# A two-layer graph network kernel on one core: every engine's order of steps and the order of the shared PSUM banks chosen anew

## The reference, cut to what matters

```
# layer 0: attention masked by adj
v, q, k = relu(x Wv + bv), relu(x Wq + bq), relu(x Wk + bk)
att = softmax((q k^T) * adj - 9e15 * (1 - adj))
x   = layernorm(x + relu((att v) Wo + bo))
# layer 1: a rank-one attention weighted by adj
h   = x W^T + b ;  e, f = h a1, h a2
u   = adj * exp(e_i + f_j + a_b)
x   = layernorm(x + (u / sum(u)) h)
```

## Time and profile before

| what | value |
|---|---|
| median of three runs | 395.15 us (395.12 to 395.23) |
| the profiled execution | 395.13 us, span 393.4 us |
| mean granted TensorE clock | 0.991 of full speed |
| busy: PE, ACT, DVE, POOL | 380.5 (97%), 329.9 (84%), 292.8 (74%), 279.9 (71%) us |
| HBM traffic | 204 GB/s over the span |

### The profile page before, as it was taken

The page is one execution under the profiler, slowest core; times in us unless marked ns, Lnnn a source line. Parts: engine busy times, 40 slices in busy tenths (PEclk is TensorE's granted clock), DMA queues, the critical chain, the costliest instruction groups (busy, mean ns, idle before and its releaser), DMA issues.

```text
span 393.4 us, 8653 instructions
## 1 busy us (share of the span) xinstructions
PE 380.5 (97%) x2757; PEld 355.2 (90%) x2757; DVE 292.8 (74%) x883; ACT 329.9 (84%) x661; POOL 279.9 (71%) x258
## 2 busy tenths in 40 slices
PE   8999999999999999999999999999999999999990
PEld 7798989989999999999999999999999999999990
DVE  3786796678668886777957887688867779697976
ACT  5877679987889887997879878898888969999962
POOL 1454951696458994789937998389956899576673
PEclk9999999999999999999999999999999999999996
DMA  8945533807657168754597266780676647978011
GB/s 259 376 166 166 164 129 137 328 38 268 200 185 314 61 235 260 262 203 171 175 292 298 84 240 215 243 322 13 253 214 233 252 162 285 386 224 282 4 55 53
DMA packets 38156, 80.71 MB, mean 205 GB/s; under 512 B 2785, under 2 KB 19681, under 8 KB 38113
## 3 DMA queue, kind: packets, MB, share of 16 engines
q1 hardware_dynamic: 37824, 80.03, 58.3%
q10 hardware_dynamic: 288, 0.14, 0.1%
HBM read 75.96 MB, written 4.19 MB: 204 GB/s over the span
## 4 chain that ended last, share of the span: by engine, by line
PE 91%; DVE 5%; issue 2%; POOL 0%; ACT 0%; POOLq 0%; DVEq 0%; ACTq 0%
PE pt_ps L1612 14%; PE m_ps L1660 13%; PE s_ps L1541 8%; PE av_ps L1625 8%; PE av_ps L1626 8%; PE av_ps L1624 8%; PE s_ps L1543 7%; PE s_ps L1542 7%; PE m_ps L1583 4%; PE m_ps L1649 3%; PE m_ps L1633 3%; PE m_ps L1541 2%; PE m_ps L1542 2%; PE m_ps L1543 2%; PE m_ps L1640 2%
## 5 line engine op out<-in xcount | busy, mean ns | idle before, releaser
L1033 DVE TENSOR_TENSOR prob_tl<-pt_ps,prob_th 128x512 fp32r<-128x512 f32 x128 | 85.5, 684 | 29.8 <-ACT prob_th L670 29.6
L1025 DVE CUSTOM_DVE_ANT_0 prob<-s_ps,penalty 128x1024 f32<-128x1024 f32 x64 | 78.0, 1218 | 30.8 <-PE s_ps L1543 26.2
L670 ACT ACTIVATE prob_th<-pt_ps 128x512 fp32r<-128x512 f32 x128 | 74.7, 596 | 21.0 <-PE pt_ps L1612 20.8
L405 POOL TENSOR_SCALAR penalty<-raw 128x1024 bf16<-128x1024 f32 x64 | 66.4, 1047 | 28.3 <-DMA raw<-in_adj_dram 13.2
L662 ACT ACTIVATE prob<-prob,neg_max 128x1024 f32<-128x1024 f32 x64 | 73.8, 1153 | 1.4 <-DVE neg_max L1025 1.3
L1624 PE MATMUL av_ps<-prob_th,vh 128*128 128x256 f32 x256 | 74.1, 290 | 0.0
L1612 PE MATMUL pt_ps<-rhs,prob 128*128 128x128 f32 x512 | 73.2, 273 | 0.0
L1626 PE MATMUL av_ps<-prob_th,vl 128*128 128x256 f32 x256 | 72.4, 283 | 0.0
L1625 PE MATMUL av_ps<-prob_tl,vh 128*128 128x256 f32 x256 | 72.4, 283 | 0.0
L607 ACT ACTIVATE adj_t<-adjt_in 128x1024 fp32r<-128x1024 f32 x56 | 59.3, 1061 | 11.2 <-PE m_ps L1660 11.1
L1612 PEld LDWEIGHTS pt_ps<-rhs,prob 128*128 128x128 f32 x512 | 60.1, 141 | 4.1
(11 more groups left out here) (139 smaller groups left out, 785.2 us busy)
## 6 DMA issues: line engine op xcount, KB each, us to landing
raw<-in_adj_dram SPq DMA_DIRECT2D x64, 512.0 KB, 5.6
adjt_in<-in_adj_t_dram SPq DMA_DIRECT2D x56, 512.0 KB, 3.9
x_in<-in_x_dram SPq DMA_DIRECT2D x8, 512.0 KB, 6.2
raw<-in_adj_t_dram SPq DMA_DIRECT2D x8, 512.0 KB, 5.7
out_dram<-out_sb SPq DMA_DIRECT2D x14, 256.0 KB, 4.5
xt_odd<-in_x_t_dram SPq DMA_DIRECT2D x8, 256.0 KB, 5.2
raw<-in_x_t_dram SPq DMA_DIRECT2D x7, 256.0 KB, 4.7
out_dram<-out_sb SPq DMA_DIRECT2D x4, 128.0 KB, 1.8
```

The costliest lines, as they stand in the source:

```text
L670: sc.activation(prob_th[n % 2][:, tiles(k), (i % 2) * P:(i % 2 + 1) * P], pt_ps[k][:, :].rearrange("p (c n) -> p c n", n=P), ACT.Copy).the ...
L1025: v.tensor_tensor_reduce(out=prob[i % 2][:, :], in0=s_ps[:, :, :].rearrange("p a n -> p (a n)"), in1=penalty[:, n % RING, :], scale=-1.0, ...
L1033: v.tensor_tensor(prob_tl[n % 2][at], pt_ps[k][:, :].rearrange("p (c n) -> p c n", n=P), prob_th[n % 2][at].bitcast(F32), ALU.subtract).th ...
```

## The change

No step, wait or buffer is added or removed. In the head, the pass and the tail, the order of each engine's list is replaced by another, and the order of the bank slots follows that of PE. What follows is cut from the diff; the lists that are not shown change in the same way. Lines without a sign stand in both.

SP, head:

```
             def head():
+                load_adj(0, 0)
                 load_x_t_quarter(0)
+                load_x_t(0, 1)
                 load_x_t_quarter(1)
-                load_x_t(0, 1)
+                load_adj(0, 4)
                 load_wb()
-                load_adj(0, 0)
+                load_x_t(1, 0)
+                load_x(0)
                 load_adj(0, 1)
-                load_x(0)
-                load_x_t(1, 0)
...
```

DVE and ACT, head:

```
             def head():                      # DVE
+                first_x_lo_quarter(0)
                 split_in(0)
-                first_x_lo_quarter(0)
                 first_x_lo_quarter(1)
                 split_in(1)
+                place_rhs1()
                 first_x_lo(1)
-                place_rhs1()
+                first_q_lo(0)
                 centre_w()
                 first_k_lo(0)
-                first_q_lo(0)
+                first_k_lo(1)
                 v_bias(0, 0)
-                first_k_lo(1)
                 v_bias(0, 1)
                 mask_max(0, 0)
...
                 q_out(0, 0)                  # ACT
+                q_hi(0, 0)
                 k_out(0, 0)
-                q_hi(0, 0)
+                k_out(0, 1)
                 k_hi(0, 0)
-                k_out(0, 1)
                 k_hi(0, 1)
```

The tail, from the last `attend` on, PE and ACT:

```
-                project_out(LAST, 2)
-                transpose_x1_pair(1)
                 project_h_pair(0)
+                project_out(LAST, 2)
                 attend(LAST, 3)
+                transpose_x1_pair(1)
                 transpose_x1_pair(2)
+                project_out(LAST, 3)
                 project_h_pair(1)
-                project_out(LAST, 3)
-                project_h_pair(2)
                 hold_clock()
-                hold_clock()
                 transpose_x1_pair(3)
-                aggregate_first(0)
-                aggregate_first(1)
+                project_h_pair(2)
+                hold_clock()
                 project_h_pair(3)
                 aggregate_first(2)
                 aggregate_first(3)
+                aggregate_first(1)
+                aggregate_third(2)
+                aggregate_first(0)
...
                 g_hi_pair(2)                 # ACT
-                round_last(7)
                 exp_ef_pair(3)
                 g_scale_pair(3)
                 g_hi_den_pair(3)
                 g_hi_pair(3)
+                norm0_pair(1)
                 norm0_pair(2)
+                round_last(7)
                 norm0_pair(3)
```

## The result

The changed kernel takes 403.83 us (403.38 to 404.11, 4 runs) against 395.19 us for the kernel before (4 runs beside it): ratio 1.0218, 95% interval 1.0200 to 1.0235, 8.64 us slower. The forecast was 396.4 us in a range of 394.6 to 398.4: the right direction, and a seventh of the size. The profiled execution has a span of 402.1 us.

What follows compares the result with a forecast made beforehand. TensorE was taken as the bound, busy nearly every microsecond from 15 us on. From 395.13 us: head +1.5, pass 1 -0.3, passes 2 to 6 +0.3, tail -0.2, giving 396.4 us, range 394.6 to 398.4.

Steps and rivals of the forecast that it cites:

- two ways in: Head: late loads of wb or x_t delay TensorE; +1.5 us taken between them, bounds +0.5 and +3.1.
- wb: Head: this load lands 3.5 us later, at 10.4, making PE's work after the second first_scores 1.1 us late.
- x_t: Head: its quarters land later behind adj(0,0), so all projections start 1.5 to 2.0 us later.
- Pass 1: Wait of scores(1,4) for mask_max(1,3) shrinks from 0.46 to 0.16 us: -0.3 us, bounds -0.5 and +0.3.
- Passes 2 to 6: Steady passes: small stalls from tight margins, 0.06 us a pass, +0.3 us for five, bounds 0 and +1.0.
- av_out behind round_adj: Passes, ACT: round_adj(p-2,5) goes ahead of av_out(p-1,3), needed by project_out(p-1,3) on PE; margin 0.1 us.
- Tail: Last batch: earlier g_lo_pair(3) against later aggregates and agg_outs; -0.2 us, bounds -1.0 and +0.6.
- g_lo_pair(3) sooner by 0.85: Tail, DVE: moving ACT's round_last(7) behind the four pairs lets this step come 0.85 us sooner.
- The passes stall: Rival, passes: ACT's margin short by 0.15 us more in each of five passes, 397.2 us; chance 0.10.
- The clock stays low longer: Rival, head: PE idles and six first_scores instructions run at the low clock, costing 1.4 us: 397.8; chance 0.13.
- The start was not hidden: Refers to the rival that the start is hidden: head loses only 0.5 us, total 395.1; chance 0.15.
- the tail did not win: Refers to the rival that the tail wins more than the head loses: gains 2.3 us with pass 1, 394.3; chance 0.10.

Runs made afterwards that it cites:

- h_wb: The changed kernel with load_wb() moved ahead of load_adj(0, 4) in SP's head: 403.71 us (1.0219).
- h_sp: The changed kernel with SP's head alone in the order before, other engines keeping the changed head: 401.16 us (1.0146).
- b_mask: The kernel before with one step of the change alone, mask_max(p,3) on DVE ahead of stats0(p-1,1): 395.15 us (1.0004).
- p_pow: The changed kernel with rstd0_pow(p-1) on POOL moved behind convert(p,5), (p,6) and (p,7) in the pass: 403.85 us (1.0208).
- t_fix: The changed kernel with DVE's end of the tail as before, plus moves of POOL, ACT and DVE steps in the tail: 402.45 us (1.0187).
- fix_end: fix_all with rstd1_pow(LAST-1) ahead of rstd0_pair(3) on POOL and DVE's steps from residual0(LAST,2) to agg_out(LAST,0) as before: 399.71 us (1.0099).
- m_head: The kernel before with only the head's order of the changed kernel, on all five engines and its row of banks: 398.04 us (1.0074).
- fix_all: The changed kernel with SP's head, TensorE's last aggregates and round_last(7) as before, plus the moves of p_pow and t_fix: 400.22 us (1.0130).

## Why the prediction was wrong

**Head: mechanism right in part, size off.** The prediction named two ways in, wb (1.1 us) and x_t (projections 1.5 to 2.0 us later), and took +1.5 "between the two ways". They do not average: both delay the same products, so the later one counts. The first projection starts 1.83 late, and the head came to +2.4, inside the bounds of +0.5 to +3.1. wb, which had most of the working, did not matter: kl waits for kh, and h_wb is no sooner. That the projections start 1.5 to 2.0 us later came out in part by luck. The late x_t alone makes TensorE wait 0.78 us, since before it had warm-up products to fill the time; 1.05 come from the split of w_a, which now stands behind a step on x_t on DVE and which the prediction did not ask about. It cost little once x_t came early (first projection at 4.91 in h_sp); no run moved it alone. The other 0.7 us, the slower products, were in a rival and not in the sum.

**Pass 1: the gap closed, for 0.12 us instead of 0.3.** b_mask shows why: behind that wait the next one, for prob_lo, is as close.

**Passes 2 to 6: this step failed, +2.6 instead of +0.3, past its bound of +1.0.** The prediction looked for steps that come late in their own queue, found av_out behind round_adj, and priced it at 0.06 us a pass. That wait exists (0.19) and costs nothing. The prediction took every duration from the trace of before as a property of the instruction. The runs show that on DVE it also depends on what POOL runs at that moment: 1.4 of the 2.6 us are one step of 8 columns that waits for POOL's conversions (p_pow). The change puts convert(p,5) to (p,7) directly behind rstd0_pow on POOL's list, and the prediction did not ask which DVE step they would then lie beside. The other 1.2 us are named only in part.

**Tail: this step failed, +3.8 instead of -0.2, past its bound of +0.6.** The step worked out, g_lo_pair(3) sooner by 0.85, happened (0.98), but the end did not wait for it. What it left out is the same as in the passes: POOL's normalisation of the batch before and add_wb, and in the first part q_lo and v_lo, lie beside DVE's small steps. t_fix got 1.9 of the 3.8 us back by moving mostly POOL's steps, and behind TensorE's last product fix_end got back all of it; in the first part the cause is in part argued.

The trace of before had the sign. Beside a POOL step of 1.19 us, a shift of 2 columns on DVE took 0.93:

```profile
368.66 1.19 POOL L454 TENSOR_TENSOR gs<-gs,x1b 128x512 f32<-128x512 f32 x1
...
368.94 0.93 DVE L1143 SCALAR_TENSOR_TENSOR shift<-mv,rstd 128x2 f32<-128x2 f32 x1
```

and the row of L1074 above has a median of 167 ns with a maximum of 931. A spread like that on a step of fixed shape was a price to look up, and it was not looked for.

**The rivals.** "The passes stall" was right in kind, but with another cause, and 2.6 us where it allowed 1.05. "The clock stays low longer" came true, at half its price and in another place: six products of 512 columns took 0.58 to 0.63 us, the last at 10.17, where before it was two, some 0.7 us in all where the rival had 1.4, but those of first_scores took 0.39 to 0.50. The start was not hidden, and the tail did not win.

## What to carry to other kernels

When an order moves steps between queues, list for each small DVE step with its operands in SBUF which of POOL's long steps runs beside it before and after; a short step whose greatest duration is many times its median says that it has been held. Where two late inputs feed the same product, take the later one, not a value between. A wait that is seen in a trace is no cost until its removal shortens the stage: two of them here (av_out, mask_max) were worth nothing.

## What the runs showed of the hardware

A DVE step whose operands both lie in SBUF did not run beside POOL's long steps (conversions, casts, subtractions of 512 columns, the normalisation); it ended with or after them: 0.97 us instead of 0.17 for 8 columns, 1.01 instead of 0.15 for 2, two residual steps 1.40 instead of 0.60. Steps that read PSUM ran on beside POOL at their usual length (agg_out 0.41 to 0.43, mask_max 1.22). So did DVE steps beside POOL's powers of 2 to 8 columns. In the kernel before, the shift of 2 columns that takes 0.93 us beside POOL's addition takes 0.13 inside a power:

```profile
374.86 1.65 POOL L464 TENSOR_TENSOR rstd<-var,minus_half 128x8 f32<-128x8 f32 x1 [0.64 <-DVE var L1118]
...
375.55 0.13 DVE L1143 SCALAR_TENSOR_TENSOR shift<-mv,rstd 128x2 f32<-128x2 f32 x1
```

The Trainium skill (SBUF — State Buffer, section SBUF: two separate sides) states a rule for it: DVE and GpSimd share a pair of ports under an exclusive lock, which a DVE instruction with two SBUF inputs needs when the GpSimd instruction reads SBUF, and whichever starts first keeps it for its whole length. The traces agree for POOL's long steps. They do not for the powers, whose operands lie in SBUF too; there the measurement decides. The section also names DVE instructions in a 2-port perf mode; whether a var of 2 columns with a single SBUF operand, 0.69 us beside POOL in the kernel before and 0.16 alone, is one, no run here tells.

TensorE's products came to full speed at different times for the same head: those of 512 columns went from 0.63 to 0.40 us at 10.60 in the changed kernel and only past 11.55 in m_head. They did so at 7.33 in the kernel before; in fix_all, which has the early projections again, the first, at 6.26, took 0.45 already. In t_fix, also with the changed head, the granted clock is 1.00 from 5.2 to 8.4, 0.50 (1.2 GHz) from 8.6 to 11.9 and 1.00 from 12.0 on; TensorE had waited from 4.77 to 6.63 before it fell.
